# Edge preparation cut to the sources, group 0's statistics ahead of the first scan, loads of x laid between stores

## The chip, the core and the metric

One core of a Trainium2 chip runs the kernel as one program. The metric is device time in microseconds, median of the runs. TensorE (PE) multiplies, VectorE (DVE), ScalarE (ACT) and GpSimd (POOL) work on SBUF and PSUM, and SyncE (SP) issues most transfers. They run side by side and meet at semaphores only.

## The reference, cut to what matters

```
xn = layernorm(x)                                   # x: 6250 x 256
Wh = xn @ W_w + W_b                                 # graph attention over 100000 edges (src, dst)
e  = leaky(Wh[dst] @ a_d + Wh[src] @ a_s + a_b)
h  = relu(segment_softmax_sum(e, Wh[dst], by=src))
k, v = phi(xn @ Wk + bk), xn @ Wv + bv              # linear attention, kv = sum over rows
x1 = x + h + mix(xn, kv)                            # two layernorms and a feed-forward
out = x1 + experts(layernorm(x1))                   # 6 experts, top 2
```

Edges come sorted by the reference's second index; the kernel has to sort them by `src` itself.

## The kernel before, in words

x lies in SBUF as 50 tiles of 125 rows (`NT`, `R`), loaded two tiles at a time in 25 loads (`NC`). Edges lie as 128 rows of 784 (`COLS`), the last row with 432 only. Stage A, on which the change works, does two things at once in 50 rounds b:

- *Counting edges by block of 125 sources.* ScalarE makes a mask of block b (`mask`, L963), three rounds ahead; VectorE scans it (`scan`, L634), and places the ranks (`place`, L641); ScalarE keeps the ends (`end`, L972).
- *Projecting tiles.* Per step s, ScalarE normalises tile s+1 and copies the turned rows of tile s out of PSUM (`turned`, L983 to L988), TensorE transposes tile s and multiplies tile s-1 (`products`, L1130, five matmul lines from L1139), VectorE reads the results (`neighbours`, L580; `values`, L587), and TensorE adds tile s-4 to kv. `steps_at(b)` (L436) says which of the 54 steps (`STEPS`) fall into round b: none in rounds 0 and 1, then 9 in 8 rounds.

`turned(t)` waits until the store of tile t-2's turned rows to `xt_rows` has landed (`xt_out`), as its buffer has two places. `products(t)` waits for `values(t-2)`. Tiles need mean and deviation first: `moments` (L647), per group of ten tiles (`SG`) `statistics` (L656), ScalarE's logarithm and exponential (L1014, L1016) and `less_mean` (L688). Loads 0 to 4 of x fill `x_in`, 5 to 14 `rows_moved[0]`, 15 to 24 `rows_moved[1]`; the first moments of a set wait for all of it. Group 0's are in round 1, after the first scans, those of `weights` (L667) behind them. `group_at(b)` names the round in which a group is finished.

Order on SyncE's queue (L441 to L466): six transfers of edges, the 25 loads of x, twelve late weights, then per tile the store of turned rows (waits for `p_tc`) and of the row of the table (waits for `p_row`). VectorE prepares both arrays of edges (L604 to L632) before ScalarE may make its first mask (`edges_ready`). GpSimd makes constants, issues the prefill of `slots`, more constants, then parts of two biases.

Behind stage A come the prefix sums on TensorE (L1161), VectorE's line L713 that waits for them, and all the rest, some 2000 us.

Of the kernel before, what the change touches and what calls it, by code (L numbers as in the profile page):

```python
# [14 lines left out]
I32 = mybir.dt.int32  # L15
F16 = mybir.dt.float16
BF16 = mybir.dt.bfloat16
U32 = mybir.dt.uint32
ALU = mybir.AluOpType
ACT = mybir.ActivationFunctionType  # L20
AX = mybir.AxisListType

N, D, E = 6250, 256, 100000
R = 125
RW = R + 1
NT = N // R
CH = 2 * R
NC = N // CH
L = 128
# [26 lines left out]
FIRST, STEPS, SG = 2, NT + 4, 10  # L56
# [71 lines left out]
def gps_kernel(nc, x, src, dst, gW, gWb, ga, gab, Wq, bq, Wk, bk, Wv, bv, Wo, bo, W1, b1, W2, b2,  # L128
# [7 lines left out]
    with ExitStack() as ctx:  # L136
# [172 lines left out]
        v0h, v1h, hih, loh = (take(COLS // 2).bitcast(F16) for _ in range(4))  # L309
# [10 lines left out]
        cumi, dhi, dlo = masks[3].bitcast(I32), cums[0].bitcast(I32), cums[1].bitcast(I32)  # L320
# [111 lines left out]
        def group_at(b):  # L432

            return (b - 1) // 5 if b % 5 == 1 and b < 5 * (NT // SG) else None

        def steps_at(b):  # L436

            first = max(0, (b - FIRST) * STEPS // (NT - FIRST))
            return range(first, max(first, (b + 1 - FIRST) * STEPS // (NT - FIRST)))

        with nc.Block() as block:  # L441
            @block.sync
            def _(sp):
                last = E - (L - 1) * COLS
                for arr, to in ((src, srci), (dst, dsti)):
                    for a, b in ((0, 112), (112, L - 1)):
                        sp.dma_start(to[a:b, :], arr[a * COLS:b * COLS].rearrange("(p c) -> p c", c=COLS)).then_inc(edges_in, 16)
                    sp.dma_start(to[L - 1:L, 0:last], arr[(L - 1) * COLS:E].rearrange("(p c) -> p c", p=1)).then_inc(edges_in, 16)
                for i in range(NC):
                    sp.dma_start(xn[:, 2 * i:2 * i + 2, :],  # L450
                                 x[CH * i:CH * (i + 1), :].rearrange("(t p) d -> p t d", p=R)).then_inc(x_in if i < SG // 2 else rows_moved[(i - SG // 2) // SG], 16)

                for to, frm in loads_late:
                    sp.dma_start(to, frm, allow_slow_non_contiguous=True).then_inc(w_late, 16)

                def keep_turned(t):
                    sp.wait_ge(p_tc, t + 1)
                    sp.dma_start(xt_rows[t // 2, :, :, (t % 2) * R:(t % 2) * R + R], xT[:, t % 2, :, :]).then_inc(xt_out[t % 2], 16)

                for t in range(2):  # L460
                    keep_turned(t)
                for t in range(NT):
                    if t + 2 < NT:
                        keep_turned(t + 2)
                    sp.wait_ge(p_row, t + 1)
                    sp.dma_start(table[t * R:(t + 1) * R, :], whs[0:R, t % 4, :]).then_inc(p_out[t % 4], 16)  # L466
# [35 lines left out]
            def _(g):  # L502
# [14 lines left out]
                g.wait_ge(const_step, 3)  # L517
                g.dma_start(slots[0:SLOTS].rearrange("(p s) -> p s", p=128), empty).then_inc(prefilled, 16)
# [51 lines left out]
            def _(dve):  # L570
# [3 lines left out]
                def step(ins):  # L574

                    n[0] += 1
                    ins.then_inc(rank_step, 1)
                    dve.wait_ge(rank_step, n[0])
# [24 lines left out]

                dve.wait_ge(edges_in, 96)  # L604
                dve.wait_ge(consts, 1)
                last = E - (L - 1) * COLS
                V.memset(srcf, float(N))
                step(V.memset(dhi, 0))
                V.tensor_copy(srcf[0:96, :], srci[0:96, :])
                V.tensor_copy(srcf[96:128, 0:last], srci[96:128, 0:last])  # L610
                step(V.tensor_copy(srcf[96:127, last:COLS], srci[96:127, last:COLS]))
                V.tensor_scalar(dhi[0:96, :], dsti[0:96, :], 10, None, ALU.logical_shift_right)
                V.tensor_scalar(dhi[96:128, 0:last], dsti[96:128, 0:last], 10, None, ALU.logical_shift_right)
                V.tensor_scalar(dhi[96:127, last:COLS], dsti[96:127, last:COLS], 10, None, ALU.logical_shift_right)
                step(V.tensor_scalar(cumi, srcf, 0.5, 1.0 / R, ALU.add, ALU.mult))
                step(V.tensor_copy(q0, cumi))
                step(V.scalar_tensor_tensor(cmp, q0, float(R), srcf, ALU.mult, ALU.is_gt))
                step(V.tensor_tensor(blk, q0, cmp, ALU.subtract))
                step(V.memset(dlo, 0))
                V.tensor_scalar(dlo[0:96, :], dsti[0:96, :], 1023, None, ALU.bitwise_and)  # L620
                V.tensor_scalar(dlo[96:128, 0:last], dsti[96:128, 0:last], 1023, None, ALU.bitwise_and)
                V.tensor_scalar(dlo[96:127, last:COLS], dsti[96:127, last:COLS], 1023, None, ALU.bitwise_and)
                step(V.scalar_tensor_tensor(srcf, blk, -float(R), srcf, ALU.mult, ALU.add))
                step(V.tensor_copy(cmp, dhi))
                step(V.tensor_scalar(srcf, srcf, 1.0, 8.0, ALU.add, ALU.mult))
                V.tensor_tensor(v1h, srcf, cmp, ALU.add)
                V.memset(wpos, 0.0)
                V.memset(bpos, -1.0e6)
                V.memset(E_[:, 0, :], 0.0)
                step(V.tensor_copy(v0h, dlo))  # L630
                V.memset(G_[:, 0:1], 0.0).then_inc(edges_ready, 1)
                dve.wait_ge(edges_ready, 1)  # L632
# [60 lines left out]

                scan(0)
                for b in range(NT):
                    i = group_at(b)
                    for t in range(0, SG) if b == 1 else range(SG + 2 * (b - 2), min(NT, SG + 2 * (b - 1))) if b > 1 else ():
                        moments(t)
                    if i is not None:
                        statistics(i)  # L700
                    if i == 0:
                        weights()
                    if b + 1 < NT:
                        scan(b + 1)
                    if i is not None:
                        less_mean(i)
                    place(b)
                    for s in steps_at(b):
                        proj(s)
                dve.wait_ge(placed, NT)  # L710

# [243 lines left out]
            def _(act):  # L955
# [5 lines left out]
                act.wait_ge(edges_ready, 1)  # L961
# [45 lines left out]
                for b in range(3):  # L1007
                    mask(b, b, b % 4, 0)
                for b in range(NT):
                    i = group_at(b)  # L1010
                    if i is not None:
                        g = slice(SG * i, SG * i + SG)
                        act.wait_ge(var_ready, 2 * i + 1)
                        A.activation(rstd_all[:, g], mvs[:, g, 1], ACT.Ln, bias=eps[0:R, :]).then_inc(rstd_ready, 1)  # L1014
                        act.wait_ge(rstd_ready, 2 * i + 1)
                        A.activation(rstd_all[:, g], rstd_all[:, g], ACT.Exp, scale=-0.5).then_inc(rstd_ready, 1)  # L1016
                    if b + 3 < NT:
                        mask(b + 3, b + 3, (b + 3) % 4, b)
                    end(b)
                    for s in steps_at(b):  # L1020
                        proj(s)
# [1360 lines left out]
```

## Time and profile before

| | |
|---|---|
| median of the runs | 2300.26 us (2300.15 to 2304.06) |
| the profiled execution, its span | 2298.15 us, 2296.4 us |
| busy share of the span | PE 83%, DVE 74%, ACT 64%, POOL 49% |
| stage A in it | 0 to about 305 us |
| granted TensorE clock | 0.926 of full |

The 40 slices of the page are 57 us each. Slice 2 (57 to 115 us) shows PE at 5 tenths and PEclk at 7, between slices at 8 and more. The timeline of single engines tells what stood still in it. Starts of one line of TensorE, which runs once for each tile, tell the pace of the stage.

### The profile page before, as it was taken

Reading aid. Unit: us, or ns where it says so; the run is one execution under the profiler, and the core shown is the slowest. Engines: PE = TensorE matmul, PEld = TensorE weight load, DVE = VectorE, ACT = ScalarE, POOL = GpSimd, SP = SyncE. Lnnn points to the kernel's source line nnn. Section 1 sums busy time; section 2 is a strip of 40 time slices with the busy share of each in tenths; the row PEclk is TensorE's granted clock in tenths of the full one; section 3 lists DMA queues with packets and bytes.
Section 4 is the critical chain, followed back from the end, with each engine's and each line's share of the span. In section 5 each row is a group of like instructions: output and inputs, shape, how many; then the busy total and the mean of one; then the engine's idle time right before and its main releaser. Section 6 shows DMA issues by size and latency. Waiting matters only on the chain. (4 is left out here: it accounts for less than half of the span.)

```text
span 2296.4 us, 50185 instructions
## 1 busy us (share of the span) xinstructions
PE 1901.7 (83%) x10177; PEld 1538.0 (67%) x10177; DVE 1709.2 (74%) x5357; ACT 1463.3 (64%) x4497; POOL 1119.3 (49%) x1107
## 2 busy tenths in 40 slices
PE   1588858699983999999999999999998572699996
PEld 0345436488872877778777788787787462588885
DVE  7687878878884888898888888988888552255543
ACT  3566739334422888899888898988988660233332
POOL 2000000011125777777777766777774277255554
PEclk9799979699995999999999999999999665799998
DMA  4312201021113444444444444444442543255553
GB/s 137 87 50 59 59 23 50 27 76 46 44 27 83 122 117 119 121 119 120 117 118 121 114 110 115 120 116 118 117 122 71 178 161 132 65 93 91 94 97 54
DMA packets 132951, 218.68 MB, mean 95 GB/s; under 512 B 41572, under 2 KB 87135, under 8 KB 132655
## 3 DMA queue, kind: packets, MB, share of 16 engines
q0 software_dynamic: 61648, 135.33, 24.5%
q1 hardware_dynamic: 66345, 72.68, 10.6%
q10 hardware_dynamic: 4662, 7.46, 1.1%
q8 instruction: 95, 1.56, 0.3%
q14 instruction: 201, 1.65, 0.2%
HBM read 153.08 MB, written 56.42 MB: 91 GB/s over the span
## 5 line engine op out<-in xcount | busy, mean ns | idle before, releaser
L1362 POOL DMA_INDIRECT area<-wh_table,area x812 | 784.2, 966 | 275.5 <-issue 242.3
L1689 PE MATMUL bank<-area 128*126 x2008 | 495.8, 389 | 41.3 <-ACT area L1602 20.8
L1689 PEld LDWEIGHTS bank<-area 128*126 128x126 f32 x2008 | 358.0, 188 | 116.6 <-issue 67.5
L1395 DVE TENSOR_SCALAR area<-iota_row,area 128x126 f32<-128x126 f32 x1004 | 358.9, 365 | 21.2 <-ACT area L1562 15.4
L1595 ACT ACTIVATE area<-iota_row,area 128x126 f32<-128x126 f32 x753 | 292.9, 389 | 0.0
L2180 POOL DMA_INDIRECT out_dram<-area x108 | 169.6, 1571 | 163.4 <-DVE area L2241 146.6
L1609 ACT ACTIVATE area<-area 128x126 f32<-128x126 f32 x753 | 242.8, 386 | 0.5
L1548 ACT ACTIVATE area<-bank 125x512 bf16<-125x512 f32 x251 | 149.0, 594 | 85.4 <-DVE area L1409 82.3
L1470 DVE SCALAR_TENSOR_TENSOR acc_mem<-acc_mem,area,bank 125x258 f32 x251 | 120.6, 480 | 100.3 <-PE bank L1677 84.1
L1709 PE MATMUL bank<-area 128*128 128x250 f32 x800 | 188.6, 379 | 6.2 <-ACT area L1616 3.5
L1665 PE MATMUL bank<-ident,area 128*126 128x128 f32 x1004 | 162.0, 284 | 33.9 <-DVE area L1395 33.8
L1720 PE MATMUL bank<-area 128*125 128x256 f32 x800 | 189.6, 380 | 0.0
L559 POOL IOTA acc_mem<- 50x812 f32 x1 | 0.8, 807 | 353.5 <-DVE area L828 353.5
L1409 DVE TENSOR_REDUCE area<-bank 125x1 f32<-125x512 f32 x251 | 171.4, 683 | 0.0
L1709 PEld LDWEIGHTS bank<-area 128*128 128x128 f32 x800 | 153.1, 192 | 26.6 <-ACT area L1616 3.9
L1720 PEld LDWEIGHTS bank<-area 128*125 128x125 f32 x800 | 150.4, 188 | 23.7
L2241 DVE SCALAR_TENSOR_TENSOR area<-bank,area 128x256 f32<-128x256 f32 x108 | 47.3, 480 | 143.3 <-PE bank L2338 77.4
L564 POOL DMA_INDIRECT sorted_slots<-area x28 | 46.0, 1641 | 216.5 <-DVE area L919 203.4
L2273 ACT ACTIVATE area<-bank,area 128x256 f32<-128x256 f32 x108 | 45.3, 471 | 139.8 <-issue 133.6
L1665 PEld LDWEIGHTS bank<-ident,area 128*126 128x126 f32 x1004 | 106.5, 141 | 39.1 <-DVE area L1395 38.7
L1880 POOL DMA_INDIRECT moe_rows<-area x100 | 99.7, 997 | 66.8 <-ACT area L2030 37.0
L1562 ACT ACTIVATE area<-area,iota_blk 128x4 f32 x251 | 74.8, 298 | 54.8 <-SPq L1354 32.4
(416 smaller groups left out, 4147.8 us busy)
## 6 DMA issues: line engine op xcount, KB each, us to landing
area<-moe_rows SPq DMA_DIRECT2D x54, 264.0 KB, 2.7
area<-wh_table,area POOLq DMA_INDIRECT x812
area<-area SPq DMA_DIRECT2D x18, 388.5 KB
wh_table<-area SPq DMA_DIRECT2D x50, 126.5 KB
xn<-in_x_dram SPq DMA_DIRECT2D x25, 250.0 KB
xt_rows<-area SPq DMA_DIRECT2D x50, 125.0 KB, 2.4
area<-xt_rows SPq DMA_DIRECT2D x25, 250.0 KB, 2.6
x_rows<-area SPq DMA_DIRECT2D x25, 250.0 KB
```

The source lines that it names most:

```text
L1362: g.indirect_dma_start(out=gath[:, (i + GT) % RS, :], out_offset=None, in_=table, in_offset=bass.IndirectOffsetOnAxis(ap=idx_tab[:, i:i + ...
L1395: ins = V.tensor_scalar(xm[:, b, t, :], iota_row[:, :], rowl[:, j % 10, t:t + 1], fetched(j, D)[:, t:t + 1], ALU.is_equal, ALU.mult)
L1409: V.tensor_reduce(gmax[0:R, b:b + 1], bank[XT[j % 2]][0:R, :], AX.X, ALU.max).then_inc(d_m, 1)
L1470: V.scalar_tensor_tensor(row, row, alpha[0:R, j % 5:j % 5 + 1], bank[US[b]][0:R, 0:WROW], ALU.mult, ALU.add).then_inc(d_acc, 1)
L1548: A.activation(hot[0:R, b, :], bank[XT[j % 2]][0:R, :], ACT.Sign).then_inc(a_hot, 1)
L1595: last = A.activation(dist[:, t, :], iota_row[:, :], ACT.Abs, bias=rowl[:, j % 10, t:t + 1], scale=-1.0)
L1609: last = A.activation(sm[:, b, t, :], dist[:, t, :], ACT.Exp, bias=e3[:, b, t:t + 1], scale=-1.0e12)
L1665: last = T.transpose(bank[XT[j % 2]][0:RW, t * L:(t + 1) * L], xm[:, b, t, :], ident[:, :])
L1689: last = T.matmul(bank[US[b]][0:RW, 0:WROW], sm[:, b, t, :], gath[:, bass.ds(place + t, 1), 0:WROW].rearrange("p a w -> p (a w)"), start=( ...
L1709: last = T.matmul(bank[HB[p % 2]][:, i * CH:(i + 1) * CH], w_1[:, k, f * 128:(f + 1) * 128], x1T[:, k, :], start=(k == 0), stop=(k == 1))
L1720: last = T.matmul(bank[AB][0:R, r * D:(r + 1) * D], hT[:, f, r * R:(r + 1) * R], w_2[:, f, :], start=(f == 0), stop=(f == 7))
L2180: g.indirect_dma_start(out=out, out_offset=bass.IndirectOffsetOnAxis(ap=rowi[:, j % RB6, s, MW - 2:MW - 1], axis=0), in_=yo[:, j % 3, s, : ...
```

## The change

Sources only are prepared ahead of the masks; the destinations' part of it is done in `destinations()` behind the last place. The edges are loaded as rows 0 to 95, 96 to 126 and 127, the last two behind two memsets of rows 96 to 127. `weights`, the moments of the first ten tiles, `statistics(0)` and `less_mean(0)` stand ahead of `scan(0)`, and ScalarE's `deviations(0)` behind its first three masks. Steps are spread over all 50 rounds. Moments of tiles 10 on begin at b = 4, groups end at b = 8, 13, 18, 23. SyncE issues nine loads of x, then the others between the stores, and the late weights at t = 16. GpSimd waits for the edges ahead of the prefill.

```diff
@@ -53,7 +53,7 @@
...
 SLOT, TAB_SLOTS = 6, 8
-FIRST, STEPS, SG = 2, NT + 4, 10
+STEPS, SG, X_FIRST = NT + 4, 10, 9
 ST, NS, PB3 = 12, 5, 3
@@ -306,7 +306,10 @@
...
         cums = [take(COLS) for _ in range(2)]
-        v0h, v1h, hih, loh = (take(COLS // 2).bitcast(F16) for _ in range(4))
+        v0h, v1h = (take(COLS // 2).bitcast(F16) for _ in range(2))
+        hilo = take(COLS)
+        hih, loh = (hilo[:, i * COLS // 2:(i + 1) * COLS // 2].bitcast(F16) for i in range(2))
+        dst_bits = hilo.bitcast(I32)
         iotaH = take(HI * WI // 2).bitcast(F16).rearrange("p (h i) -> p h i", i=WI)
@@ -317,7 +320,7 @@
...
         srcf, q0, cmp = masks[0:3]
-        cumi, dhi, dlo = masks[3].bitcast(I32), cums[0].bitcast(I32), cums[1].bitcast(I32)
+        cumi, dhi = masks[3].bitcast(I32), cums[0].bitcast(I32)
         lpi, lpt = masks[0].bitcast(I32), masks[1].bitcast(I32)
@@ -431,27 +434,28 @@
...
-            return (b - 1) // 5 if b % 5 == 1 and b < 5 * (NT // SG) else None
+            return (b - 3) // 5 if b % 5 == 3 and SG // 2 < b < 5 * (NT // SG) else None
...
-            first = max(0, (b - FIRST) * STEPS // (NT - FIRST))
-            return range(first, max(first, (b + 1 - FIRST) * STEPS // (NT - FIRST)))
+            return range(b * STEPS // NT, (b + 1) * STEPS // NT)
...
                 last = E - (L - 1) * COLS
-                for arr, to in ((src, srci), (dst, dsti)):
-                    for a, b in ((0, 112), (112, L - 1)):
-                        sp.dma_start(to[a:b, :], arr[a * COLS:b * COLS].rearrange("(p c) -> p c", c=COLS)).then_inc(edges_in, 16)
-                    sp.dma_start(to[L - 1:L, 0:last], arr[(L - 1) * COLS:E].rearrange("(p c) -> p c", p=1)).then_inc(edges_in, 16)
-                for i in range(NC):
+                def load_x(i):
                     sp.dma_start(xn[:, 2 * i:2 * i + 2, :],
...
-                for to, frm in loads_late:
-                    sp.dma_start(to, frm, allow_slow_non_contiguous=True).then_inc(w_late, 16)
+                for arr, to in ((src, srci), (dst, dsti)):
+                    sp.dma_start(to[0:96, :], arr[0:96 * COLS].rearrange("(p c) -> p c", c=COLS)).then_inc(edges_in, 16)
+                for arr, to in ((src, srci), (dst, dsti)):
+                    sp.wait_ge(edges_ready, 1)
+                    sp.dma_start(to[96:L - 1, :], arr[96 * COLS:(L - 1) * COLS].rearrange("(p c) -> p c", c=COLS)).then_inc(edges_in, 16)
+                    sp.dma_start(to[L - 1:L, 0:last], arr[(L - 1) * COLS:E].rearrange("(p c) -> p c", p=1)).then_inc(edges_in, 16)
+                for i in range(X_FIRST):
+                    load_x(i)
@@ -459,9 +463,16 @@
...
                     keep_turned(t)
+                    load_x(X_FIRST + 2 * t)
+                    load_x(X_FIRST + 2 * t + 1)
                 for t in range(NT):
...
                         keep_turned(t + 2)
+                    if X_FIRST + 4 + t < NC:
+                        load_x(X_FIRST + 4 + t)
+                    if t == NC - X_FIRST:
+                        for to, frm in loads_late:
+                            sp.dma_start(to, frm, allow_slow_non_contiguous=True).then_inc(w_late, 16)
                     sp.wait_ge(p_row, t + 1)
@@ -515,6 +526,7 @@
...
                 g.wait_ge(const_step, 3)
+                g.wait_ge(edges_in, 96)
                 g.dma_start(slots[0:SLOTS].rearrange("(p s) -> p s", p=128), empty).then_inc(prefilled, 16)
@@ -600,36 +612,30 @@
...
                         keys(s - 3)
-
+                last = E - (L - 1) * COLS
+                V.memset(srci[96:128, last:COLS], N)
+                V.memset(dsti[96:128, last:COLS], 0).then_inc(edges_ready, 1)
                 dve.wait_ge(edges_in, 96)
                 dve.wait_ge(consts, 1)
-                last = E - (L - 1) * COLS
-                V.memset(srcf, float(N))
-                step(V.memset(dhi, 0))
-                V.tensor_copy(srcf[0:96, :], srci[0:96, :])
-                V.tensor_copy(srcf[96:128, 0:last], srci[96:128, 0:last])
-                step(V.tensor_copy(srcf[96:127, last:COLS], srci[96:127, last:COLS]))
-                V.tensor_scalar(dhi[0:96, :], dsti[0:96, :], 10, None, ALU.logical_shift_right)
-                V.tensor_scalar(dhi[96:128, 0:last], dsti[96:128, 0:last], 10, None, ALU.logical_shift_right)
-                V.tensor_scalar(dhi[96:127, last:COLS], dsti[96:127, last:COLS], 10, None, ALU.logical_shift_right)
+                step(V.tensor_copy(srcf, srci))
+                V.memset(wpos, 0.0)
                 step(V.tensor_scalar(cumi, srcf, 0.5, 1.0 / R, ALU.add, ALU.mult))
+                V.memset(E_[:, 0, :], 0.0)
                 step(V.tensor_copy(q0, cumi))
+                V.memset(G_[:, 0:1], 0.0)
                 step(V.scalar_tensor_tensor(cmp, q0, float(R), srcf, ALU.mult, ALU.is_gt))
                 step(V.tensor_tensor(blk, q0, cmp, ALU.subtract))
-                step(V.memset(dlo, 0))
-                V.tensor_scalar(dlo[0:96, :], dsti[0:96, :], 1023, None, ALU.bitwise_and)
-                V.tensor_scalar(dlo[96:128, 0:last], dsti[96:128, 0:last], 1023, None, ALU.bitwise_and)
-                V.tensor_scalar(dlo[96:127, last:COLS], dsti[96:127, last:COLS], 1023, None, ALU.bitwise_and)
                 step(V.scalar_tensor_tensor(srcf, blk, -float(R), srcf, ALU.mult, ALU.add))
-                step(V.tensor_copy(cmp, dhi))
-                step(V.tensor_scalar(srcf, srcf, 1.0, 8.0, ALU.add, ALU.mult))
-                V.tensor_tensor(v1h, srcf, cmp, ALU.add)
-                V.memset(wpos, 0.0)
-                V.memset(bpos, -1.0e6)
-                V.memset(E_[:, 0, :], 0.0)
-                step(V.tensor_copy(v0h, dlo))
-                V.memset(G_[:, 0:1], 0.0).then_inc(edges_ready, 1)
-                dve.wait_ge(edges_ready, 1)
+                V.tensor_scalar(v1h, srcf, 1.0, 8.0, ALU.add, ALU.mult).then_inc(edges_ready, 1)
+                dve.wait_ge(edges_ready, 2)
+
+                def destinations():
+                    step(V.tensor_scalar(dst_bits, dsti, 10, None, ALU.logical_shift_right))
+                    step(V.tensor_copy(v0h, dst_bits))
+                    step(V.tensor_tensor(v1h, v1h, v0h, ALU.add))
+                    step(V.tensor_scalar(dst_bits, dsti, 1023, None, ALU.bitwise_and))
+                    step(V.tensor_copy(v0h, dst_bits))
+                    step(V.memset(bpos, -1.0e6))
@@ -691,15 +697,18 @@
...
+                weights()
+                for t in range(SG):
+                    moments(t)
+                statistics(0)
+                less_mean(0)
                 scan(0)
...
                     i = group_at(b)
-                    for t in range(0, SG) if b == 1 else range(SG + 2 * (b - 2), min(NT, SG + 2 * (b - 1))) if b > 1 else ():
+                    for t in range(SG + 2 * (b - 4), min(NT, SG + 2 * (b - 3))) if b >= 4 else ():
                         moments(t)
...
                         statistics(i)
-                    if i == 0:
-                        weights()
                     if b + 1 < NT:
@@ -708,6 +717,7 @@
...
                 dve.wait_ge(placed, NT)
+                destinations()
@@ -958,7 +968,7 @@
...
                 act.wait_ge(consts, 1)
-                act.wait_ge(edges_ready, 1)
+                act.wait_ge(edges_ready, 2)
@@ -1006,14 +1016,17 @@
...
                     mask(b, b, b % 4, 0)
+                def deviations(i):
+                    g = slice(SG * i, SG * i + SG)
+                    act.wait_ge(var_ready, 2 * i + 1)
+                    A.activation(rstd_all[:, g], mvs[:, g, 1], ACT.Ln, bias=eps[0:R, :]).then_inc(rstd_ready, 1)
+                    act.wait_ge(rstd_ready, 2 * i + 1)
+                    A.activation(rstd_all[:, g], rstd_all[:, g], ACT.Exp, scale=-0.5).then_inc(rstd_ready, 1)
+
+                deviations(0)
                 for b in range(NT):
-                    i = group_at(b)
-                    if i is not None:
-                        g = slice(SG * i, SG * i + SG)
-                        act.wait_ge(var_ready, 2 * i + 1)
-                        A.activation(rstd_all[:, g], mvs[:, g, 1], ACT.Ln, bias=eps[0:R, :]).then_inc(rstd_ready, 1)
-                        act.wait_ge(rstd_ready, 2 * i + 1)
-                        A.activation(rstd_all[:, g], rstd_all[:, g], ACT.Exp, scale=-0.5).then_inc(rstd_ready, 1)
+                    if group_at(b) is not None:
+                        deviations(group_at(b))
                     if b + 3 < NT:
```

## Rows read from the trace of the kernel before

**Rows 1.** Waits of 0 to 360 us: total us, times, longest.

```profile
ACT acc_mem L966 <- DVE area L631: 23.4, 1, 23.4
...
ACT area L988 <- DMA xt_rows<-area: 19.2, 1, 19.2
...
DVE area L713 <- ACT area L1027: 9.5, 1, 9.5
```

**Rows 2.** Timeline of SyncE's queue and L988: start, us, engine, line, operation.

```profile
3.21 56.52 SPq L450 DMA_DIRECT2D xn<-in_x_dram  x25
...
59.78 1.94 SPq L454 DMA_DIRECT2D area<-in_L_mix_Wq_dram  x1
...
69.21 5.22 SPq L458 DMA_DIRECT2D xt_rows<-area  x3
...
73.52 0.37 ACT L988 COPY area<-bank 128x250 f32<-128x250 f32 x1 [19.20 <-DMA xt_rows<-area]
```

**Rows 3.** Timeline of TensorE, starts of L1139, 0 to 300 us.

```profile
46.45 2.04 PE L1139 MATMUL bank<-area 128*125 128x512 f32 x2
...
51.80 1.02 PE L1139 MATMUL bank<-area 128*125 128x512 f32 x2
...
75.17 2.04 PE L1139 MATMUL bank<-area 128*125 128x512 f32 x2 [19.95 <-DVE area L591]
...
82.45 1.09 PE L1139 MATMUL bank<-area 128*125 128x512 f32 x2 [0.80 <-DVE area L591]
...
86.97 1.09 PE L1139 MATMUL bank<-area 128*125 128x512 f32 x2 [0.58 <-ACT area L988]
...
105.00 1.09 PE L1139 MATMUL bank<-area 128*125 128x512 f32 x2 [0.57 <-ACT area L988]
...
111.11 1.09 PE L1139 MATMUL bank<-area 128*125 128x512 f32 x2 [2.18 <-DVE area L591]
...
117.25 1.09 PE L1139 MATMUL bank<-area 128*125 128x512 f32 x2 [0.57 <-ACT area L988]
...
297.97 1.09 PE L1139 MATMUL bank<-area 128*125 128x512 f32 x2 [0.79 <-DVE area L591]
```

**Rows 4.** Windows: busy us of each engine (instructions), PEclk, DMA share, GB/s.

```profile
4.00:6.00 2.00, 0.00 (x0) 0.00 (x0) 0.00 (x0) 0.00 (x0) 1.92 (x9) 1.00 1.11 264
18.00:20.00 2.00, 0.00 (x0) 0.00 (x0) 1.97 (x4) 0.00 (x0) 1.84 (x3) 1.00 0.34 120
60.00:80.00 20.00, 4.83 (x7) 1.99 (x8) 5.27 (x13) 5.63 (x14) 4.59 (x7) 0.50 0.56 142
```

**Rows 5.** DMA issues of 0 to 100 us: KB each, median us to landing.

```profile
xn<-in_x_dram SPq DMA_DIRECT2D x25, 250.0 KB
xt_rows<-area SPq DMA_DIRECT2D x8, 125.0 KB, 2.4
```

**Rows 6.** Timeline of 0 to 50 us, VectorE and ScalarE.

```profile
9.22 0.71 DVE L607 MEMSET acc_mem<- 128x784 f32 x1 [9.22 <-DMA acc_mem<-in_dst_dram]
...
31.92 3.35 DVE L652 BATCH_NORM_STATS2 area<-xn 125x6 f32<-125x256 f32 x10
...
35.30 0.18 DVE L658 TENSOR_TENSOR area<-area 125x10 f32<-125x10 f32 x1
...
36.64 0.17 DVE L665 TENSOR_SCALAR area<-area 125x10 f32<-125x10 f32 x1
...
40.32 0.16 DVE L685 TENSOR_TENSOR acc_mem<-acc_mem,area 128x1 f32<-128x1 f32 x1
...
44.51 1.09 ACT L980 ACTIVATE area<-xn,area 125x256 f32<-125x256 f32 x2
...
45.99 0.75 DVE L652 BATCH_NORM_STATS2 area<-xn 125x6 f32<-125x256 f32 x2 [2.57 <-DMA xn<-in_x_dram]
```

**Rows 7.** Timeline around a usual step, VectorE.

```profile
86.96 0.75 DVE L652 BATCH_NORM_STATS2 area<-xn 125x6 f32<-125x256 f32 x2
...
90.35 0.42 DVE L585 TENSOR_TENSOR area<-bank,area 125x259 f32<-125x259 f32 x1
```

## The prediction, made before the changed kernel ran

> **What bounds the kernel now.** I read the longest waits of the first 360 us first, then what the SyncE queue issues in that stretch, then the start of one matmul line in time. The waits [rows 1] show one large one inside the stage: ScalarE stands 19.2 us ahead of its copy of turned rows (L988) for a DMA to xt_rows, and VectorE and TensorE stand behind ScalarE. The SyncE queue [rows 2] says why: the 25 loads of x take it from 3.21 to 59.73 us, the late weights to 69.2, and only then does the first store of turned rows go out, so that L988 runs at 73.52. Nothing is slow there; the store stands behind loads that nobody needs yet.
>
> The starts of L1139, first matmul of a tile's products, are the clock of the stage [rows 3]. Tile 0 is at 46.45, tile 1 at 51.80, tile 2 at 75.17 (the hole), tile 3 at 82.45, tile 4 at 86.97, tile 49 at 297.97. The usual step is 4.51 us: 40 of the 45 steps from tile 4 on lie at 4.50 to 4.52; the other five are three of 6.1 us (105.00 to 111.11 is one), in which VectorE has the statistics of a group of ten tiles as well, and two of 6.15 (111.11 to 117.25 is one), each right behind such a step, in which TensorE was slower itself. Behind the hole, where the granted clock was 0.50, 1.2 GHz [rows 4], the first pair of L1139 takes 2.04 us against 1.09. Check: 45 x 4.51 = 203.0, 3 x 1.60 and 2 x 1.63 give 211.0, and 297.97 - 86.97 = 211.0. Inside a usual step VectorE and TensorE take turns: products, then neighbours and values (L584 to L591) read them, then the next products. All that follows needs this stage complete, so a time saved at tile 49 should be saved at the end, one for one; I argue this from the order of the code.
>
> **Where the stage starts.** Now VectorE waits for all edges until 9.22, prepares both arrays, and ScalarE's first mask waits 23.4 us for it [rows 1, 6]. The tile statistics come after the first scan and normalising starts at 44.51. In the changed kernel the order is sources, weights, statistics of group 0, scan 0. What is late next is not the edges but x: statistics of group 0 need loads 0 to 4. Their landing isn't in the trace, but load 14's is: VectorE's first record after waiting for it is at 45.99 [rows 6]. The loads run at 120 GB/s, 0.34 of the 16 DMA engines being busy [rows 4], so 250 KB [rows 5] take 2.12 us each, and load 4 landed at about 45.99 - 10 x 2.12 = 24.8.
>
> **The edges' new cut.** Rows 0 to 95 of both arrays go first, rows 96 to 126 as transfers of 31 rows, where it was 112 and 15. The trace has no 31-row transfer. Bounds from rows: transfers of many rows run with all engines busy, 264 GB/s at a share of 1.11 (counted as over full), the 125-row loads of x with a third of them [rows 4]. 125 is 5 x 25 and 5 of 16 is 0.31; the number of rows seems to decide how many engines carry it, and 31 has no divisor. Lower end: 31 rows go as well as 112, cost 0 (no reason for a gain, the bytes are equal). Upper end: one engine carries all 31. That engine then has 29 rows more of each array (6 + 31 against 7 + 1); a row is 784 words of 4 bytes, so 182 thousand bytes at 120.5 / 5 = 24.1 GB/s, 7.5 us. Loads of x stand behind them on the same queue and are complete only when that engine's part is. I take the upper end: the nearest row is the load of x, an odd count of rows. Load 4 then lands at 24.8 + 7.5 = 32.3.
>
> The Trainium skill, DMA: Bandwidth & Descriptors, section Why a DMA increments its semaphore by 16 and not by 1, says that a transfer uses the largest number up to 16 that divides the slowest dimension of both sides, so that 125 rows get 5 engines and 31 rows one. The share of 0.34 agrees for 125; no row here shows it for 31. By it the sum is 2287, by equal spreading 2279.
>
> **What the opening costs after that.** By the same count the edges are in at about 17 us at worst (9.2 + 7.5); both arrays take VectorE some 16 us now, from 9.22 to its release of ScalarE, and the sources with fewer memsets well under half of it, 6 to 7, to about 24; the weights take 3.7 (from the end of L665 at 36.81 to that of L685 at 40.48, [rows 6]), to about 28. All of it is hidden under the wait for load 4, and costs up to its length if x came earlier: the prepared sources would have to be late by 4 us more. GpSimd now waits for the edges ahead of its prefill, with its iotas and the bias parts behind it; that is about 10 us of work and nobody needs it before products start at about 42, so 0. From x's landing: ten moments 3.35, eight small operations 1.5 (35.30 to 36.81), and ScalarE's two and less_mean, at the 0.2 of such a one and their handoffs, 0.8 [rows 6]: 5.6 in all. Scan 0 starts at T = 32.3 + 5.6 = 37.9. The scan and ScalarE's copy of its ends take about 2.1 (estimated), and 1.94 from normalising to L1139 (44.51 to 46.45) [rows 3, 6] put tile 0's products at T + 4.0 = 41.9; it was 46.45.
>
> **The stall that goes, and the one that comes.** Stores of turned rows now go out between loads, and the 19.2 us are gone. But tile 10's moments, at b = 4, wait for one semaphore that loads 5 to 14 fill, and load 14 is now issued only after tile 3's turned rows. Who is first? VectorE reaches b = 4 at about T + 15.4: products of tile 1 end at about T + 14 (4.0 + 5.35 + a full step), and VectorE's reads behind them are four operations of up to 0.42 (L585, [rows 7]). Load 9 starts at about T + 5.5 (turned rows of tile 0 at T + 3.9, one store ahead); loads 9 to 13 take 5 x 2.12, the stores between them 2.4 (one of the table at 120 GB/s, 1.0, three of turned rows, 125 KB each [rows 5], at 264 GB/s, 0.47), then load 14's 2.12 and about 0.9 for the landing: T + 21.5. So VectorE stands 6.1 us, and queued behind it are scan 5, place 4, and the reads for which products 3 wait. From the start of moments to the next L1139 it is one usual step, 4.51 (the row at 86.96 to 91.47, [rows 3, 7]). Products of tile 3 start at T + 26.0 = 63.9, against 82.45: 18.5 earlier.
>
> From there to tile 49 the same 46 steps, 207.5. Statistics of a group fall into usual steps four times now (groups 1 to 4) where three did before, 4 x 1.60 = 6.4; the lower clock followed in two of three, so 2.7 x 1.63 = 4.4. After the hole of some 7 us TensorE starts slow: tile 2's step was 7.28 instead of 4.51 and tile 0's 5.35 [rows 3]; I take 2.4. Together 220.7, tile 49 at 284.6, against 297.97: 13.4 earlier. More steps per round (54 over 50 rounds, not over 48) costs nothing, since the step is bound by products.
>
> The other edits. The loads of late weights, 9.4 us of issue [rows 2], now stand at t = 16 with the table's store 16 and turned rows 19 behind them; tile 21's copy waits for the latter, some 13 us on, so 0, at most 3. The destinations' six operations, about 4 us, come after the last place, where VectorE now idles 9.5 us for the sums (L713, [rows 1]): 0, up to 4 if that cover is gone. Second wait for x at b = 14 (loads 15 to 24): load 24 is issued when turned rows of tile 13 are there, lands some 5.2 us later, and VectorE comes 5.1 after them: 0 to 1.
>
> **The sum.** Span 2296.4 - 13.4 = 2283.0; 1.75 lie around the span (2298.15 in all): 2284.8; the runs' median is 2.1 above that execution: 2286.9.
>
> **Rivals.** (1) *31 rows spread well*: everything 7.5 earlier, 2279.4. For it: equal bytes, short rows. Against: the 0.34. Chance 0.12. (2) *No new stall at b = 4*: the loads come as VectorE does, by a quicker queue or a later VectorE; minus 6.1 and the 2.4 of clock, 2278.4. Against: six loads at 2.12 are 12.7 us alone. Chance 0.12; both together 2271. (3) *A second stall at b = 14*, or behind the late weights, of the size of the first, 6 and 2.4: 2295.3. For it: my margin there is 0.1 us. Chance 0.14. (4) *Slower*: the wait of turned rows for the store two tiles before (xt_out) takes the place of the removed one. Ahead of each store on its queue there is now a load of 2.12 and a table store of about 1. It decides from a landing of two steps, 9.0 us after issue; the median was 2.4 [rows 5], and 4.3 behind the loads (69.21 to 73.52, [rows 2]). At 10.7 it would lengthen some 11 steps by 1.7, 18.7 in all: 2305.6. Against: the five engines' need is 3.5 us per step of 4.51. Chance 0.07. The forecast's own case has 0.55.
>
> **Numbers.** A measurement can tell 0.2%, 4.6 us: faster is below 2295.7, slower above 2304.9. Faster: 0.53 of the forecast's case, both 0.12, half of rival 3: 0.83 or 0.84; the rest of these, 0.10, within; slower 0.07. The range leaves out rival 4, the far half of rival 3 and both gains together: 2273 to 2296.
>
> **What would show it.** The changed trace should have no wait of L988 for xt_rows over 1 us; statistics of tile 0 at about 32 (25 if rival 1 holds); tile 0's products at 42; a wait of about 6 us of VectorE's moments for x at some 53 to 59; four long steps; the last L1139 at 285; and the distance from there to the end as before. The prediction is wrong if the loads between the stores lengthen usual steps beyond 4.51, or if the stages behind don't move along.

## The result, and the profile of the changed kernel

The changed kernel takes 2284.9 us (median of 10 runs) against 2300.2 for the kernel before beside it: ratio 0.9935, interval 0.992 to 0.9951, so 15 us or 0.65% faster. The forecast was 2287, in a range of 2273 to 2296. In the profiled execution the span is 2282.1 us; the sum had 2283.0. One execution of the kernel with both repairs, below, took 3817.4 us where its four others took 2265.2 to 2268.0, and its ratio leaves that one out.

The waits of the first 345 us of the changed kernel (engine, tile, line, releaser: us in total, times, longest) answer to [rows 1]:

```profile
ACT acc_mem L976 <- DVE acc_mem L629: 21.9, 1, 21.9
...
PE bank L1152 <- DVE area L603: 19.6, 8, 9.6
...
DVE acc_mem L620 <- DMA acc_mem<-in_dst_dram: 16.0, 1, 16.0
...
DVE area L658 <- DMA xn<-in_x_dram: 10.7, 3, 8.7
...
DVE area L723 <- ACT area L1040: 5.7, 1, 5.7
```

No wait of ScalarE for xt_rows is left, where it was 19.2 us. What is new is VectorE's wait for x, 10.7 us in three parts, 8.7 of it in one, and TensorE's 9.6 for VectorE behind it. VectorE's wait at L723 for the sums fell from 9.5 to 5.7: the destinations' operations lie in it.

The timeline of the opening (start, us, engine, line, operation) answers to [rows 2, 6]:

```profile
17.67 0.57 DVE L620 CAST acc_mem<-acc_mem 128x784 f32<-128x784 int32 x1 [16.00 <-DMA acc_mem<-in_dst_dram]
...
28.22 0.16 DVE L691 TENSOR_TENSOR acc_mem<-acc_mem,area 128x1 f32<-128x1 f32 x1
...
29.54 3.37 DVE L658 BATCH_NORM_STATS2 area<-xn 125x6 f32<-125x256 f32 x10 [1.16 <-DMA xn<-in_x_dram]
...
35.27 3.47 DVE L645 TENSOR_TENSOR_SCAN acc_mem<-ones,acc_mem 128x784 f32<-128x784 f32 x2
...
39.06 0.62 SPq L462 DMA_DIRECT2D xt_rows<-area  x1
...
50.47 0.65 SPq L448 DMA_DIRECT2D xn<-in_x_dram  x1
...
58.32 0.75 DVE L658 BATCH_NORM_STATS2 area<-xn 125x6 f32<-125x256 f32 x2 [8.73 <-DMA xn<-in_x_dram]
```

VectorE waits 16.00 us for the edges and has them at 17.67, the weights are through at 28.38 (28.22 and 0.16), x's first five loads have landed at 29.54, scan 0 is at 35.27. The store of turned rows at 39.06 now goes out while loads of x are still to come; before, the first waited for all of them [rows 2]. Load 14, the last that the semaphore of loads 5 to 14 counts, is issued at 50.47; VectorE sees it at 58.32, having stood 8.73 us.

The starts of L1152, the line that was L1139 [rows 3]:

```profile
39.18 2.04 PE L1152 MATMUL bank<-area 128*125 128x512 f32 x2
...
45.20 1.02 PE L1152 MATMUL bank<-area 128*125 128x512 f32 x2
...
49.55 1.09 PE L1152 MATMUL bank<-area 128*125 128x512 f32 x2 [0.93 <-DVE area L603]
...
62.65 2.04 PE L1152 MATMUL bank<-area 128*125 128x512 f32 x2 [9.61 <-DVE area L603]
...
70.06 1.09 PE L1152 MATMUL bank<-area 128*125 128x512 f32 x2 [0.58 <-ACT area L998]
...
79.08 1.09 PE L1152 MATMUL bank<-area 128*125 128x512 f32 x2 [0.57 <-ACT area L998]
...
85.17 1.48 PE L1152 MATMUL bank<-area 128*125 128x512 f32 x2 [2.16 <-DVE area L603]
...
91.28 1.09 PE L1152 MATMUL bank<-area 128*125 128x512 f32 x2 [0.58 <-ACT area L998]
...
285.31 1.09 PE L1152 MATMUL bank<-area 128*125 128x512 f32 x2 [0.79 <-DVE area L603]
```

Tile 0 is 7.3 us earlier than before, tile 3 is at 62.65 against 82.45, and tile 49 at 285.31 against 297.97: 12.66 us. Of the 19.8 us at tile 3 the stage gives 7.1 back before its end: 2.9 in the step behind the hole (62.65 to 70.06 is 7.41, a usual step 4.51), 1.6 in a fourth step with a group's statistics (79.08 to 85.17 is one, 6.09; before there were three), 1.6 more in slow steps behind such (three, where there were two; 85.17 to 91.28 is one, 6.11), 1.1 in small ones (read below). The stage behind it starts at 315.34 (ScalarE's first L1106) against 328.01 for the same line before, there L1093, 12.67 earlier; the span is 14.3 shorter. The other 1.6 us arise behind the stage and lie within what executions of one kernel differ by, 2278.8 to 2292.9 here. So I read small effects from tile 49's products, not from the span.

### The profile page after: what moved, and what is told of

Its sections match the earlier page's. It is cut to its first block and busy times, and to the rows that moved or that the text cites. A ratio compares the mean times of both kernels' runs of the same rounds, so it can differ in the third digit from the quotient of the medians.

```text
span 2282.1 us, 50180 instructions
## 1 busy us (share of the span) xinstructions
PE 1906.9 (84%) x10177; PEld 1541.7 (68%) x10177; DVE 1701.8 (75%) x5350; ACT 1463.4 (64%) x4497; POOL 1124.2 (49%) x1107
## 5 line engine op out<-in xcount | busy, mean ns | idle before, releaser
L1251 PE MATMUL bank<-area 128*128 128x128 f16 x784 | 104.7, 298 | 5.0 <-DVE area L929 5.0
```

## The experiments

Two numbers are read of each kernel: the start of the last tile's products in the profiled execution (285.31 in the changed kernel), and the runs' median. Line numbers shift by a few between them; the tile and the operation tell which line it is.

### The 31 rows as 16 and 15

```diff
-                    sp.dma_start(to[96:L - 1, :], arr[96 * COLS:(L - 1) * COLS].rearrange("(p c) -> p c", c=COLS)).then_inc(edges_in, 16)
+                    for a, b in ((96, 112), (112, L - 1)):
+                        sp.dma_start(to[a:b, :], arr[a * COLS:b * COLS].rearrange("(p c) -> p c", c=COLS)).then_inc(edges_in, 16)
...
-                dve.wait_ge(edges_in, 96)
+                dve.wait_ge(edges_in, 128)
```

> The changed kernel with the 31 rows of each array of edges loaded as 16 and 15 rows. Theory (one DMA engine carries a transfer of 31 rows): edges are in at 9 to 10 us instead of 17, tile 0's moments start at about 25 instead of 29.5, all of the stage comes 4 to 5 us earlier (tile 49's products at 281 instead of 285.3), about 2280. The second wait for x, 8.7 us in the changed kernel, stays within 1 us. Rival (the 31 rows spread well and the edges are late since they are issued behind the memsets and beside the weights): edges still at about 17, moments at 29.5, no change, 2285.

Measured: 2273.9 us, ratio to before 0.9898 (0.9869 to 0.9927). From its waits and its timeline:

```profile
DVE area L659 <- DMA xn<-in_x_dram: 12.2, 3, 9.3
...
DVE acc_mem L621 <- DMA acc_mem<-in_dst_dram: 9.5, 1, 9.5
```

```profile
23.79 3.36 DVE L659 BATCH_NORM_STATS2 area<-xn 125x6 f32<-125x256 f32 x10 [1.92 <-DMA xn<-in_x_dram]
...
29.52 3.47 DVE L646 TENSOR_TENSOR_SCAN acc_mem<-ones,acc_mem 128x784 f32<-128x784 f32 x2
...
33.43 2.04 PE L1153 MATMUL bank<-area 128*125 128x512 f32 x2
...
52.93 0.75 DVE L659 BATCH_NORM_STATS2 area<-xn 125x6 f32<-125x256 f32 x2 [9.31 <-DMA xn<-in_x_dram]
```

VectorE waits 9.5 us for the edges where it waited 16.0, moments start at 23.79 against 29.54, and tile 49's products are at 277.10, 8.2 us earlier than in the changed kernel. The transfers of 31 rows were what held the opening back. The second wait for x stays as it was, 9.31: it moves with scan 0. The gain is larger than the 5.75 of the start: tile 3 to 4 takes 6.18 and not 7.41, and the step behind the first group's statistics 4.51 and not 6.11. With the start that is 8.6, less 0.4 elsewhere. These two terms, 2.8 us together, go with TensorE's clock: granted were 0.68 in the first of these steps (57 to 63 us) and 1.00 in the second (78 to 83), against 0.58 (62 to 70) and 0.72 (85 to 91) in the changed kernel. They are not due to the cut: the next run, with an edge tail that lands as early, has 7.36 and 6.11 in the same two places.

The windows of 12 to 14 us (busy us of each engine and count, PEclk, DMA share, GB/s; here of SyncE alone, so clock, share and GB/s) show the same from the transfers' side, first the changed kernel from 12 to 14, then this one:

```profile
12.00:14.00 2.00, 1.00 0.18 59
```

```profile
12.00:14.00 2.00, 1.00 0.67 250
```

In the changed kernel the transfers in flight move only 59 GB/s on 0.18 of the engines then, while loads of x are queued that move 120 when alone [rows 4]. Had only one of five engines been taken from the loads, the other four could have moved 96 (an estimate, four fifths of 120). So more was held back than that one engine's part; what held it back no view shows. In this run the prefill falls into that window too, so its 250 GB/s are not all x.

### The 31 rows as 30 and 1

```diff
-                    for a, b in ((96, 112), (112, L - 1)):
+                    for a, b in ((96, L - 2), (L - 2, L - 1)):
```

(against the kernel of the run above)

> The changed kernel with the 31 rows as 30 and 1, a number of rows with small divisors instead of a prime. Theory (the divisors of the number of rows set how many DMA engines carry a transfer): 30 rows spread over many, edges in at about 10, tile 0's products at about 33.5, tile 49 at 277 as with 16 and 15 rows. Rival (any tail that isn't 16 rows or its multiple is slow, or the second transfer's size decides): edges at 16 to 17, tile 0's products at 39.

Measured, in a single run: 2280.0 us.

```profile
DVE area L659 <- DMA xn<-in_x_dram: 11.2, 3, 8.7
...
DVE acc_mem L621 <- DMA acc_mem<-in_dst_dram: 8.2, 1, 8.2
```

```profile
22.59 3.37 DVE L659 BATCH_NORM_STATS2 area<-xn 125x6 f32<-125x256 f32 x10 [1.97 <-DMA xn<-in_x_dram]
...
32.23 2.04 PE L1153 MATMUL bank<-area 128*125 128x512 f32 x2
```

The edges' wait is 8.2, tile 0's products are at 32.23, tile 49's at 278.22, 1.1 later than with 16 and 15 in spite of the earlier start, by the two slower steps. In these two executions 30 rows and one are in a little sooner than 16 and 15; that one row inside the same transfer costs 7.8 us of waiting (16.0 less 8.2). The bytes are the same in all three, and a transfer of 30 rows is hardly smaller than one of 31: neither its size nor the place in the queue makes the wait, but the number of its rows. The Trainium skill, DMA: Bandwidth & Descriptors, section Why a DMA increments its semaphore by 16 and not by 1, gives 31 rows one engine and 30 rows fifteen; these runs agree in what it leads to, though no view here counts the engines of one transfer.

### Loads 5 to 9 counted apart

```diff
-                                 x[CH * i:CH * (i + 1), :].rearrange("(t p) d -> p t d", p=R)).then_inc(x_in if i < SG // 2 else rows_moved[(i - SG // 2) // SG], 16)
+                                 x[CH * i:CH * (i + 1), :].rearrange("(t p) d -> p t d", p=R)).then_inc(x_in if i < SG // 2 else slots_in if i < SG else rows_moved[(i - SG // 2) // SG], 16)
...
+                    elif SG <= t < 2 * SG:
+                        dve.wait_ge(slots_in, 16 * (SG // 2))
                     elif t >= SG:
-                        dve.wait_ge(rows_moved[(t - SG) // (2 * SG)], 16 * SG)
+                        dve.wait_ge(rows_moved[(t - SG) // (2 * SG)], 16 * ((SG // 2, SG)[(t - SG) // (2 * SG)]))
```

The later waits on both semaphores are set to the new counts.

> The changed kernel, but tiles 10 to 19 wait for loads 5 to 9 only (another semaphore, free at that time, counts them), not for loads 5 to 14. Theory (the wait of 8.7 us is for load 14 and nothing else of the stage is that late): VectorE's wait at the fifth round is under 1 us, TensorE has no hole and doesn't restart slowly, tile 49's products at 285.3 - 8.7 - 2.9 = 273.7, about 2273. Rival (behind it the stores of turned rows are as late, because loads of x stand ahead of them): ScalarE then waits for xt_rows or the next products come late, a gain of under 4 us.

Measured: 2272.3 us, ratio 0.9893 (0.9866 to 0.992). Its waits for x, and starts of L1154:

```profile
DVE area L660 <- DMA xn<-in_x_dram: 1.9, 2, 1.4
```

```profile
54.04 1.09 PE L1154 MATMUL bank<-area 128*125 128x512 f32 x2 [0.90 <-DVE area L603]
...
130.19 2.04 PE L1154 MATMUL bank<-area 128*125 128x512 f32 x2 [2.18 <-ACT area L1007]
...
137.91 1.09 PE L1154 MATMUL bank<-area 128*125 128x512 f32 x2 [0.58 <-ACT area L1000]
```

Windows (busy us of each engine, PEclk, DMA share, GB/s) of TensorE in the step of tile 18, which is behind the third group's statistics: this run first, then the changed kernel, where it starts at 141.53 behind a stop of 2.18 us:

```profile
130.00:138.00 8.00, 7.23 (x16) 0.57 0.51 104
```

```profile
141.00:146.00 5.00, 3.94 (x15) 1.00 0.84 154
```

The wait at the fifth round is gone (1.9 us are left in all, 1.4 of it before tile 0), tile 3's products are at 54.04 against 62.65, and no other wait takes its place: 8.6 us. With the restart behind the hole, 2.9, that would be 11.5 at tile 49; measured are 7.3 (278.00). The missing 4.2 are in two steps: 130.19 to 137.91 and the one at 157.55, each behind a step with statistics, took 7.72 and 7.69, where the changed kernel has 4.51 and 6.20, 4.7 more; the rest is a few tenths the other way. The granted clock says what they are: 0.57 from 130 to 138, so mostly the lower level of 1.2 GHz, against 1.00 in the changed kernel, and the first pair of the line takes 2.04 us for 1.09. Right before, TensorE did the same in both, a stop of 2.18 us for the statistics. Why the clock falls behind some of these stops, and for how long, no run here settles. The theory holds for the wait; for the clock it had no term.

### Fifteen loads first

```diff
-STEPS, SG, X_FIRST = NT + 4, 10, 9
+STEPS, SG, X_FIRST = NT + 4, 10, 15
```

> The changed kernel with 15 loads of x ahead of the first store of turned rows instead of nine. Theory (the wait of 8.7 us at the fifth round is made by stores and gates between loads 9 and 14, not by VectorE's order): load 14 lands at about 48, the wait is gone or under 1 us; the first stores stand behind some loads, so tile 2 or 3 comes up to 4 us late; tile 49's products at 278 to 281, about 2277. Rival (the queue of loads is then in front of the first stores as in the kernel before, and ScalarE waits for xt_rows as long as VectorE did for x): no gain, tile 49 at 285.

Measured: 2277.8 us, ratio 0.9905 (0.9883 to 0.9927).

```profile
ACT area L998 <- DMA xt_rows<-area: 10.2, 5, 7.0
...
DVE area L658 <- DMA xn<-in_x_dram: 1.0, 1, 1.0
```

Both theories were partly right. VectorE's wait at the fifth round is gone, and ScalarE's for xt_rows is back, at 10.2 us in five parts, the longest 7.0. Loads and stores stand in one queue, and which go first decides who waits. But ScalarE's wait is the cheaper here: tile 3's products are at 59.59 against 62.65, tile 4's at 64.10 against 70.06, since no slow step follows, and tile 49's at 277.05, 8.3 us earlier. Not all of this is the wait's: 3.1 are there at tile 3 and 2.9 come in the step behind it, but 1.6 are a slow step that is missing behind the first group's statistics (the clock again), and 0.7 are usual steps at tiles 20 and 21, where the changed kernel has two longer ones. The late weights hang on X_FIRST too (`t == NC - X_FIRST`) and go out at t = 10 here, not 16.

### The kernel before, with SyncE's order alone changed

```diff
-                for i in range(NC):
+                for i in range(X_FIRST):
+                    load_x(i)
-                for to, frm in loads_late:
-                    sp.dma_start(to, frm, allow_slow_non_contiguous=True).then_inc(w_late, 16)
...
                 for t in range(2):
                     keep_turned(t)
+                    load_x(X_FIRST + 2 * t)
+                    load_x(X_FIRST + 2 * t + 1)
```

Here X_FIRST is 15. The rest of the loads, and the late weights (so at t = 10), stand in the loop over tiles as in the changed kernel; the opening is that of the kernel before.

> The kernel before with SyncE's order alone changed: 15 loads of x first, the other ten between the stores, late weights with tile 10; preparation, statistics and rounds as before. Theory (the removed stall is the whole gain, and the opening's reorder is eaten by the new cut and the new wait for x): tile 1 stays at 51.8, tile 2 comes at about 56.5 instead of 75.2, tile 49 at about 279, 2280 to 2282: at least as fast as the whole change. Rival (the opening's reorder carries its share): tile 49 at 288 or later, 2289.

Measured: 2281.3 us, ratio 0.9933 (0.9908 to 0.9957). Its starts of L1146:

```profile
47.21 2.04 PE L1146 MATMUL bank<-area 128*125 128x512 f32 x2
...
52.17 1.02 PE L1146 MATMUL bank<-area 128*125 128x512 f32 x2
...
59.86 1.09 PE L1146 MATMUL bank<-area 128*125 128x512 f32 x2 [4.27 <-DVE area L598]
...
66.00 1.10 PE L1146 MATMUL bank<-area 128*125 128x512 f32 x2 [1.00 <-ACT area L1002]
...
70.51 1.09 PE L1146 MATMUL bank<-area 128*125 128x512 f32 x2 [0.58 <-ACT area L995]
...
281.70 1.09 PE L1146 MATMUL bank<-area 128*125 128x512 f32 x2 [0.78 <-DVE area L598]
```

Tile 2's products are at 59.86, where 56.5 was expected: TensorE stands 4.3 us for VectorE there, since the first rounds are now paced by VectorE's opening work. Tile 49's are at 281.70, 16.3 us earlier than before and 3.6 earlier than with the whole change, so the queue's order alone gives more in these profiles than the change's net 12.66. Where does the change lose it? It leads by 8.0 us at tile 0 (39.18 against 47.21) and 3.35 at tile 3 (62.65 against 66.00), but by 0.45 at tile 4 (70.06 against 70.51): the new wait for load 14 and the slow restart behind it take back what the reordered opening gives. From there it loses 4.06 more: the first group's statistics lie in a usual step (6.09) with a slow one behind (6.11), 3.2 together, where here they lie where TensorE waits anyway, and 0.7 at tiles 20 and 21 and 0.35 at tile 11, 4.2 by these. Of the 3.6 in all, the 1.6 of that slow step are TensorE's clock and say nothing for either order. The medians, 2281.3 and 2284.9, differ as the profiles do, though their intervals against before overlap.

### The destinations ahead of the first scan again

```diff
+                destinations()
                 weights()
...
                 dve.wait_ge(placed, NT)
-                destinations()
```

> The changed kernel with the six operations on the destinations, 3.9 us, ahead of the first scan again. Theory (VectorE had only 1.2 us to spare ahead of x's landing at 29.5): scan 0 comes 2.7 later, tile 49's products at 288, about 2288. Rival (x is what the opening waits for, the destinations hide under it): within 0.5 of 285.3.

Measured: 2286.8 us, ratio 0.995 (0.9934 to 0.9966).

```profile
32.54 3.36 DVE L658 BATCH_NORM_STATS2 area<-xn 125x6 f32<-125x256 f32 x10
...
38.26 3.48 DVE L645 TENSOR_TENSOR_SCAN acc_mem<-ones,acc_mem 128x784 f32<-128x784 f32 x2
...
42.17 2.04 PE L1152 MATMUL bank<-area 128*125 128x512 f32 x2
```

No wait stands ahead of the moments now, so x is no longer last there; scan 0 is at 38.26, 3.0 later, tile 49 at 288.59, 3.3 later. The same edit with the repaired cut of edges:

> The repaired cut of edges (16 and 15 rows) with the destinations' six operations, 3.9 us, ahead of the first scan. VectorE had 1.9 us to spare ahead of x in the run with the repaired cut. Theory (what counts is the slack to x's landing): scan 0 comes 2.0 later than there (31.5 against 29.5), tile 49's products at 279. Rival (with edges in at 9.5 all preparation hides under the loads of x, so preparing sources alone is worth nothing): scan 0 at 29.5.

Measured, in a single run: 2277.5 us.

```profile
31.14 3.47 DVE L646 TENSOR_TENSOR_SCAN acc_mem<-ones,acc_mem 128x784 f32<-128x784 f32 x2
```

Scan 0 is at 31.14 against 29.52, tile 49 at 279.17 against 277.10. So taking the destinations out of the opening is worth 2 to 3 us of the stage, less than the 3.9 that they take, since part of these lies under the landing of x. In the medians, 2284.9 and 2286.8, it can't be told from nothing.

### Both repairs

> Both repairs of the changed kernel in one: the edges' tail as 16 and 15 rows, and loads 5 to 9 counted apart. Theory (two separate losses): tile 0's products at 33.4 as with the first repair, no hole at the fifth round as with the second, tile 49 at 33.4 + 238.5 (278.0 - 39.5, the second repair's run) = 272, about 2267 to 2269. Rival (one repair gives what the other would have given, as TensorE or the clock takes the rest): tile 49 at 277, 2273.

Measured: 2267.6 us, ratio to before 0.9865 (0.9846 to 0.9885), the fastest of all kernels here.

```profile
32.28 2.04 PE L1155 MATMUL bank<-area 128*125 128x512 f32 x2
...
269.06 1.09 PE L1155 MATMUL bank<-area 128*125 128x512 f32 x2 [0.79 <-DVE area L604]
```

Tile 49's products are at 269.06: 28.9 us earlier than before, 16.25 earlier than in the changed kernel. The repairs gave 8.2 and 7.3 alone and 16.25 together: two separate losses. The slow steps are part of all three numbers, so the sum's closeness says less than that the edges' wait is 8.8 us here and VectorE waits 1.6 us for x in all. Tile 49 beats the 272 of the theory by 2.9, mostly by 1.1 at tile 0 and by 1.5 in the step of tile 18, 6.18 here and 7.72 in the run that the sum was made from.

The other parts of the reorder (statistics of group 0 ahead of scan 0, steps over all rounds, the prefill behind the edges) were not run singly, so what each of them gives is not shown.

## Why the prediction was right

**The removed stall.** As argued: L988's wait is gone, and the run with SyncE's order alone gives its price, 16.3 us of the stage.

**The edges' new cut.** The choice of the upper end was right in kind. Edges were in at 17.67 (forecast about 17), weights through at 28.38 (28). Too large was what it costs x: 7.5 us by 24.1 GB/s; the two runs differ by 29.54 - 23.79 = 5.75. The rate of 24.1 GB/s was taken from five engines that each carry 25 rows of x, and a lone one did better, or a part lay beside other transfers; which, the views don't tell. Load 4 came at 29.54 and not 32.3, scan 0 at 35.27 and not 37.9, tile 0 at 39.18 and not 41.9: the forecast has all three some 2.7 too late. This term makes 1.75 of load 4's 2.76. The other 1.0 is the base: without the 31-row transfers the sum had load 4 at 24.8, and the run with 16 and 15 rows has it at 23.79. By the run with 30 and 1, 22.59, it is the other way round, 0.55 the term's and 2.2 the base's; so both terms were too large, and how they share the 2.76 is open.

**The new wait.** Named with its place, tile and semaphore, and with x at T + 21.5 against VectorE at T + 15.4, 6.1 us. Measured from T = 35.27: x at T + 23.05, VectorE at T + 14.3 (58.32 less 8.73), 8.73 us. Of the 2.6 missed, 1.5 lie on the loads' side: I let six loads follow each other without a gap, but those behind tile 1's gate came late, and the engines were down to a share of 0.22 then (the window below, 41 to 43 us, of the changed kernel). The other 1.1 is VectorE's: the products of tile 1 started at T + 9.9 (45.20) and were done at about T + 13.2, where VectorE's reads start (48.44), and I had them end at T + 14.

```profile
41.00:43.00 2.00, 1.00 0.22 63
```

**From tile 3 on.** 63.9 was forecast and 62.65 measured. The rest was forecast as 220.7 and took 222.66. Four long steps of 6.1 came as said. Slower steps came behind three of them (91.28, 121.88 and 172.56), 1.60, 1.59 and 1.69, 4.9 for 4.4. Behind the hole the step was 7.41, 2.9 for 2.4. Two terms I did not have. One is steps of 4.92 and 4.78 at tiles 20 and 21, 0.7 together, where GpSimd's bias parts, released late by the late weights, ran beside VectorE: two scans took 1.89 and 2.04 us there, where the usual one takes 1.77. The other is 4.86 at tile 11, 0.35, in which VectorE stands 0.38 ahead of L603 for nothing that the profile shows; the two kernels with the destinations ahead have the same rounds and not this step, so its cause is open.

The second of the long scans, with the GpSimd operation that started before it:

```profile
151.32 0.72 POOL L559 TENSOR_TENSOR area<-area 3x256 f32<-3x256 f32 x1
151.65 2.04 DVE L645 TENSOR_TENSOR_SCAN acc_mem<-ones,acc_mem 128x784 f32<-128x784 f32 x1
```

The kernel with both repairs, where one line's cast on GpSimd took 0.39 with no scan beside it, and 1.90 when a scan had just started, which kept its 1.77:

```profile
127.12 0.39 POOL L556 CAST area<-area 3x256 bf16<-3x256 f32 x1 [104.54 <-DMA area<-in_L_mix_b_dram]
...
129.62 1.77 DVE L646 TENSOR_TENSOR_SCAN acc_mem<-ones,acc_mem 128x784 f32<-128x784 f32 x1
129.68 1.90 POOL L556 CAST area<-area 3x256 bf16<-3x256 f32 x1
```

So it isn't enough that GpSimd runs beside a scan: in these rows the one that started second is the longer. A GpSimd operation's own span is a rough measure, and no kernel here leaves the bias parts out.

**Covers.** The destinations lie in VectorE's idle time at the end, as said (9.5 became 5.7). The second wait for x at b = 14 was 0.76 us, within 0 to 1. The late weights behind t = 16 delayed no copy of turned rows.

**One for one.** 12.66 us at tile 49 became 12.67 at the next stage's start and 14.3 in that span.

**The sum.** 13.4 forecast, 12.66 measured at tile 49. It is closer than its terms, and this is luck. The start came 2.6 earlier than forecast (T at 35.27, not 37.9). Against it stand 1.4 from T to tile 3 (27.38 for 26.0, as load 14 came 1.5 late) and 2.0 from tile 3 to 49 (222.66 for 220.7), which together are 0.7 more than the start gave. Of the 2.6 that the new wait was too short, the 1.1 by which VectorE came sooner cost nothing. What I missed is what the change costs itself. I priced the cut and the wait and took both as given; by the repairs they are 16 of the 29 us that the reorder offers. Rival 1 (31 rows spread well) and rival 2 (no new stall) fell, and with them the gains that they held: the repaired kernels show what each would have been, 277.10 and 278.00 at tile 49. Rival 3's second stall was 0.76 us, not 6. Rival 4, copies that wait for stores, appeared only with 15 loads first, and there it is smaller than the wait that it replaces.

## What to carry to other kernels

Look at how many rows a transfer has before cutting it: 31 rows as one transfer held the edges back by 6.5 to 7.8 us against the same bytes as 16 and 15 or as 30 and 1. When loads are laid between stores, look for the semaphore that counts several loads: the consumer waits for the last of them, which now hangs on the stage's own progress; count apart what is needed first. And try each part of such a change alone: here the queue's order alone gave 16.3 us of the stage and all parts together 12.7, though 1.6 of the difference is the clock's.

## What the runs showed of the hardware that was not expected

While the 31-row transfers were under way, everything in flight moved 59 GB/s on 0.18 of the engines (12 to 14 us), where loads of x move 120 GB/s at 0.34 when nothing is ahead of them. TensorE's step behind a stop of 2.2 us is not one figure: 4.51, 6.1 to 6.2 or 7.7 us, at a granted clock of 1.00, of 0.72 (85 to 91 us of the changed kernel, below) and of 0.57, in kernels that do the same in that place. This alone moves the stage by some 4 us between kernels, and is left open. And a scan of VectorE's that started inside an operation of GpSimd's took 2.04 us for 1.77, while a scan that started just before GpSimd's cast kept its 1.77 and the cast took 1.90 for 0.39.

```profile
85.00:91.00 6.00, 5.54 (x15) 0.72 0.36 102
```
